# Four streams in place of three in a software-pipelined kernel of eight layers

## The reference

```python
x = x + L0_attn(layernorm(x))   # geo: 8 heads, causal, a geometric term in the scores
x = x + L0_ffn(layernorm(x))    # 8 experts, 128 -> 512 -> 128, relu, the best one by centroid
x = x + L1_attn(layernorm(x))   # "differential": per token, 32x32 scores between its own heads;
                                # itself a block with two norms and a 512-wide feed-forward
x = x + L1_ffn(layernorm(x))    # 128x128 product of values quantised in blocks of 32
x = x + L2_attn(layernorm(x))   # LoRA attention, 16 heads, no mask
x = x + L2_ffn(layernorm(x))    # 14 experts, 128 -> 256 -> 128, gelu, router
x = x + L3_attn(layernorm(x))   # wide: 16 heads with 128-deep q and k, causal
x = x + L3_ffn(layernorm(x))    # 8 experts, 128 -> 128 -> 128, relu, with a capacity
```

## Time and profile before

| what | value |
|---|---|
| median of three runs | 3041.17 us (3022.04 to 3044.92) |
| the profiled execution | 3002.18 us |
| span in its profile, first to last instruction | 3001.0 us |
| instructions | 42829 |
| PE, PEld busy | 2090.2 us (70%), 1445.4 us (48%) |
| DVE, ACT, POOL busy | 1728.2 us (58%), 1143.4 us (38%), 665.1 us (22%) |
| mean granted clock of PE | 0.787 of 2.4 GHz |
| DMA | 200.32 MB, mean 67 GB/s |

### The profile page before, as it was taken

The page is one execution under the profiler, slowest core; times in us unless marked ns, Lnnn a source line. Parts: engine busy times, 40 slices in busy tenths (PEclk is TensorE's granted clock), DMA queues, the critical chain, the costliest instruction groups (busy, mean ns, idle before and its releaser), DMA issues. The chain is left out here.

```text
span 3001.0 us, 42829 instructions
## 1 busy us (share of the span) xinstructions
PE 2090.2 (70%) x13457; PEld 1445.4 (48%) x13457; DVE 1728.2 (58%) x4326; ACT 1143.4 (38%) x2744; POOL 665.1 (22%) x904
## 2 busy tenths in 40 slices
PE   4530775689856895589847895689858895578483
PEld 3330542456443653457444654457445654354352
DVE  2346548565765668465765667465856667453132
ACT  0320432355433553245323553245324552254251
POOL 2015013401251014300250014200250024200101
PEclk9775875699667996789678986789678976897695
DMA  6120141203040313213140313212140503211402
GB/s 179 43 71 0 22 118 36 80 20 116 25 137 15 96 43 92 82 32 104 30 140 7 113 37 95 67 57 80 38 134 1 129 29 90 59 22 33 139 1 59
DMA packets 263737, 200.32 MB, mean 67 GB/s; under 512 B 28708, under 2 KB 236964, under 8 KB 262980
## 3 DMA queue, kind: packets, MB, share of 16 engines
q1 hardware_dynamic: 257348, 184.77, 22.1%
q0 software_dynamic: 6144, 12.60, 1.4%
HBM read 151.18 MB, written 35.49 MB: 62 GB/s over the span
## 5 line engine op out<-in xcount | busy, mean ns | idle before, releaser
L1230 ACT ACTIVATE mid_room<-ps 128x512 f32<-128x512 f32 x256 | 153.1, 598 | 171.9 <-PE ps L940 171.6
L1184 ACT ACTIVATE late_room<-ps 128x384 f32<-128x384 f32 x256 | 125.7, 491 | 210.1 <-PE ps L865 206.7
L1196 ACT ACTIVATE late_room<-ps,late_neg_max 128x128 f32<-128x128 f32 (+1 forms) x512 | 186.7, 420 | 22.2 <-DVE late_neg_max L1566 19.3
L1031 PE MATMUL ps<-mid_pool 128*128 128x128 f32 x544 | 122.4, 361 | 91.2 <-DMA mid_pool<-moe_small 64.9
L1589 DVE TENSOR_REDUCE mid_room<-ps 128x2 f32<-128x512 f32 x256 | 163.8, 686 | 37.2 <-PE ps L927 34.5
L1565 DVE TENSOR_REDUCE late_neg_max<-ps 128x1 f32<-128x128 f32 x256 | 73.9, 289 | 188.8 <-PE ps L857 188.7
L938 PE MATMUL ps<-mid_pool 48*128 48x256 bf16 x512 | 164.9, 322 | 21.1 <-DVE max_rows L1604 20.3
L940 PE MATMUL ps<-max_rows,of_unit 96*128 96x256 bf16 x512 | 166.9, 326 | 0.0
L855 PE MATMUL ps<-late_aT,heads_T 128*128 128x256 f32 x512 | 162.5, 401 | 0.0
L1743 DVE TENSOR_TENSOR early_pool<-ps,early_pool 128x1024 f32<-128x1024 f32 x128 | 150.7, 1219 | 15.5 <-ACT early_pool L1286 11.2
L1268 ACT ACTIVATE mid_room<-ps,mid_pool 128x128 f32<-128x128 f32 x272 | 85.2, 364 | 183.9 <-PE ps L1031 183.4
...
...
## 6 DMA issues: line engine op xcount, KB each, us to landing
mid_pool<-in_m_w_dram SPq DMA_DIRECT2D x272, 128.0 KB, 2.1
early_pool<-m_folded_w SPq DMA_DIRECT2D x88, 256.0 KB, 3.2
early_pool<-in_m_w_dram SPq DMA_DIRECT2D x88, 256.0 KB, 3.1
...
mid_room<-moe_sorted_in SPq DMA_DIRECT2D x32, 256.0 KB, 3.0
moe_sorted_out<-mid_room SPq DMA_DIRECT2D x32, 256.0 KB, 2.4
```

The costliest lines, as they stand in the source:

```text
L1031: mm = pe.matmul(ps[:, B + b % h_banks, c * P:(c + 1) * P], table[:, c * P:(c + 1) * P], rows_T[s][:, b, :], start=True, stop=True)
L1196: ins = act.activation(probs[s][:, n % RING, qt, 0:w], ps[:, bank, qt * P:qt * P + w], ACT.Exp, bias=neg_max[s][:, n % RING, qt:qt + 1])
L1230: act.activation(probs_T[s][:, n % (2 * QUAD), :], ps[:, B + slots.index(("unit", n)) % S_BANKS, :], ACT.Exp)\
```

## The change

Four streams. EARLY keeps the geo attention and `MOE0`; the new SECOND has the differential attention, its feed-forward and the quantised layer; MID keeps LoRA and `MOE2`; LATE is as it was. Banks: EARLY 0 and 1 (one for scores), SECOND 2, MID 3 and 4, LATE 5 to 7. Turns: E, ES, ESM, five of ESML in the loop, SML, ML, L: eleven. New orders of steps are written for each, 313 letters for ESML: 58 of EARLY, 72 of SECOND, 102 of MID, 81 of LATE. Beside it:

- `geo_q` has two tiles with four heads each, like `geo_k`; scores take 17 rows of each at the head's strip. The strip copies and POOL's memset go.
- q, k and v of a tile are copied to SBUF by ACT (ring of three); DVE reads them there, and takes each quarter's reduction right behind its product.
- The values' tile `v_pad` is packed; the last stream's out tiles are placed elsewhere.
- A whole table per expert lies in DRAM; one DMA fetches it, and three tables are in flight. The tables of `MOE2` and `MOE3` are laid out by copies that ACT issues in the preparation; SP waits for them at the end of the first turn.
- The group's input is loaded at the start of the turn in which EARLY takes it; `x_next` goes.
- ACT keeps the values' product of a quad behind the next exponential, not ahead of it.

The diff, cut to its core ("..." marks what is left out):

```diff
-TABLES = 4
-TABLE_DMAS = 3
+TABLES = 3
...
+    def score_banks(self, at):
+        return self.banks if at is LORA else self.banks - 1
...
-EARLY = Stream("early", 0, 3, ["geo_in", "geo_out", "moe0_router", "diff_in", "diff_out"],
-               ["v", "o", "conn"])
-MID = Stream("mid", 3, 2, ["diff_ff", "mx_in", "lora_in", "lora_out", "moe2_in"], ["ff", "mx", "v", "o"])
+EARLY = Stream("early", 0, 2, ["geo_in", "geo_out", "moe0_router"], ["v", "o"])
+SECOND = Stream("second", 2, 1, ["diff_in", "diff_out", "diff_ff", "mx_in"], ["conn", "ff", "mx"])
+MID = Stream("mid", 3, 2, ["lora_in", "lora_out", "moe2_in"], ["v", "o"])
 LATE = Stream("late", 5, 3, ["wide_in", "wide_out", "moe3_router"], ["v", "o"])
-STREAMS = (EARLY, MID, LATE)
-S_BANKS = 2
+STREAMS = (EARLY, SECOND, MID, LATE)
...
+        first_copies = table_copies(MOE0, None, a["m0_w2"], None, a["m0_b2"])
+        later_copies = (table_copies(MOE2, a["m2_w1"], a["m2_w2"], a["m2_b1"], a["m2_b2"])
+                        + table_copies(MOE3, a["m3_w1"], a["m3_w2"], a["m3_b1"], a["m3_b2"]))
...
             @block.scalar
             def _(act):
...
+                act.wait_ge(weights_here, LOADED)
+                for dst, src in later_copies:
+                    with nc.allow_non_contiguous_dma(reason="columns of tables, once"):
+                        act.dma_start(dst, src).then_inc(later_tables, 16)
...
-                    sp.dma_start(tables[s][:, i, 0:m.w2_at], layer1[m][:, bass.ds(expert, 1), :]).then_inc(here, 16)
-                    sp.dma_start(tables[s][:, i, m.w2_at:m.b2_at],
-                                 layer2[m][:, bass.ds(expert * m.chunks, m.chunks), :]).then_inc(here, 16)
-                    sp.dma_start(tables[s][:, i, m.b2_at:m.width],
-                                 small[m][bass.ds(expert * P, P), :]).then_inc(here, 16)
+                    sp.dma_start(tables[s][:, i, :].unsqueeze(1), whole[m][:, bass.ds(expert, 1), :]).then_inc(here, 16)
...
-                if load_from is not None:
-                    sp.dma_start(x_next[:, :, :], load_from).then_inc(x_here, 16)
+                if EARLY in streams:
+                    sp.dma_start(x[EARLY][:, :, :], load_from).then_inc(x_here, 16)
+                    sp.wait_ge(x_here, 16)
...
                 def score_bank(s, at, lag, kind, n):
...
-                    if k >= S_BANKS:
-                        before_kind, before_n = slots[k - S_BANKS]
+                    ring = s.score_banks(at)
+                    if k >= ring:
+                        before_kind, before_n = slots[k - ring]
...
                     def qkv(t):
-                        if t >= 2:
-                            pe.wait_ge(qkv_used, t - 1)
-                        pe.matmul(ps[:, B + t % 2, 0:3 * DIM], aT[s][:, t * P:(t + 1) * P], diff_w[:, :],
+                        if t >= 1:
+                            pe.wait_ge(qkv_kept, t)
+                        pe.matmul(ps[:, B, 0:3 * DIM], aT[s][:, t * P:(t + 1) * P], diff_w[:, :],
...
                     for c in range(DIFF_FF // P):
-                        if c >= 2:
-                            pe.wait_ge(dh_kept, c - 1)
-                        pe.matmul(ps[:, B + c % 2, :], diff_w1[:, c * P:(c + 1) * P], aT[s][:, :],
+                        if c >= 1:
+                            pe.wait_ge(dh_kept, c)
+                        pe.matmul(ps[:, B, :], diff_w1[:, c * P:(c + 1) * P], aT[s][:, :],
...
-                            for rows, h in strips_of(b):
-                                ins = act.activation(geo_q[rows, h, :], ps[rows, B + b % s.banks, :], ACT.Copy)
...
-                    pool.memset(geo_q[:, :, :], 0.0).then_inc(geo_q_free, 1)
...
-                        k = diff_k[:, t % 2, :].rearrange("p (j d) -> p j d", d=DIFF_D).unsqueeze(1)
-                        q = ps[:, B + t % 2, 0:DIM].rearrange("p (i d) -> p i d", d=DIFF_D)
+                        q = diff_qkv[:, t % QKV_RING, 0:DIM].rearrange("p (i d) -> p i d", d=DIFF_D)
+                        k = diff_qkv[:, t % QKV_RING, DIM:2 * DIM].rearrange("p (j d) -> p j d", d=DIFF_D)
...
         with nc.Block(no_gpsimd_drain=True) as block:
-            group_block(block, [EARLY, MID], x_v[:, 2 * TILES:3 * TILES, :],
-                        None)
+            group_block(block, [EARLY, SECOND], x_v[:, TILES:2 * TILES, :], None)
+        next_turn()
+        with nc.Block(no_gpsimd_drain=True) as block:
+            group_block(block, [EARLY, SECOND, MID], x_v[:, 2 * TILES:3 * TILES, :], None)
         next_turn()
         with nc.Fori(0, GROUPS - 3) as g:
             with nc.Block(no_gpsimd_drain=True) as block:
-                group_block(block, [EARLY, MID, LATE], x_v[:, bass.ds(g * TILES + 3 * TILES, TILES), :],
+                group_block(block, list(STREAMS), x_v[:, bass.ds(g * TILES + 3 * TILES, TILES), :],
                             out_v[:, bass.ds(g * TILES, TILES), :])
             next_turn()
         with nc.Block(no_gpsimd_drain=True) as block:
-            group_block(block, [EARLY, MID, LATE], None,
-                        out_v[:, (GROUPS - 3) * TILES:(GROUPS - 2) * TILES, :])
+            group_block(block, [SECOND, MID, LATE], None, out_v[:, (GROUPS - 3) * TILES:(GROUPS - 2) * TILES, :])
```

389 lines of the change are left out of this document (193 added, 196 removed).

## The result

| | before | after |
|---|---|---|
| median, us | 3025.95 (3007.43 to 3047.53, 20 runs) | 3052.55 (3029.11 to 3070.38, 20 runs) |
| ratio, 95% interval | | 1.008 (1.0056 to 1.0098) |
| span of the profiled execution | 3001.0 | 3055.9 |

The account below looks back on a forecast made before the run. No engine was full; DVE's work stood in each turn's last third, when PE's was nearly gone. Preparation and turns summed to 2713 us, 2714 with 1.2 around, scaled by 1.013 to 2750; range 2610 to 2930.

Parts of the forecast that it names:

- E's single bank: First attention's scores wait for the previous unit's exponentials: 20 us in E alone, 5 in ES, nothing in ESML.
- Rival C: Slower: E's single score bank stalls PE in the written order, 75 us a full turn, scaled total 3128; chance 0.05.
- E, 150 forecast: Turn of EARLY alone: chain 123.9, input load 2.7, bank wait 20, turn's end and barrier 3, together 150 us.
- Tables, "nothing": Expert tables held, four to three: fetch lands in 2.1 us, under two blocks, so no cost; 6.8 us if cover goes.
- The full turn, 285 forecast: ESML turn: 1.27 times M's 226.4 us chain is 287, lessened to 285; five make 1425 us.
- ESM, SML, ML: Partial turns around the loop: ESM 248 us, SML 255, ML 226.
- Preparation, 78: Laying out whole tables in DRAM adds 8 us to 70, bounds 0 and 33, as copies may share engines with the store.
- v from SBUF, bounds of 0.1 us: DVE's reads of q, k, v from SBUF: same 1218 ns as PSUM, within 0.1 us each, 2 us a turn either way.
- the chains of M: Stream chain lengths after the change: M 226.4 us, L 152.9, S 142.1.
- FF's single bank: Four feed-forward products lose double buffering: three waits for ACT of about 1 us, 3 us of PE queue, inside the 285.
- B: Full turn stays 325 us, as one written order makes streams wait behind S's DVE pairs; scaled total 2951; chance 0.21.
- Rival A: PE never short of work, clock near full: full turn some 260 us, scaled total 2601; chance 0.17.

Follow-up runs that it names:

- the fourth run: The changed kernel with E on banks 5 to 7, two for scores, in the turns without LATE: 3005.02 against 3039.16 us for the kernel before, ratio 0.9895.
- the best kernel: Changed kernel plus 128-row scores, two E score banks without LATE, v side by side, later tables issued by SP, four tables for MID and LATE: 2821.30 us, ratio 0.931.
- The orders' run: Changed kernel with twelve full ESML turns in six written step orders, each twice, outputs not the reference's: turns of 322.3 to 413.4 us.

## Why the prediction was wrong

By size the step that failed is the length of the full turn, 206 of the 343 us that the trace is over the sum; its cause is in part open. The terms come in the order in which a cause could be shown.

**The missing term: the rows of the scores.** I took "scores take 17 rows of each" as a change of layout, and counted only its gains (the strip copies and the memset). Its cost was on the path: 2.35% in the kernel before, 3.0% the other way in the changed one. The earlier trace rows showed the scores' loop at the full clock with 128-row operands, and I carried the durations over to another form. Of the causes that an edit shows, this is the largest.

**E's single bank, mis-sized.** The mechanism was right, the size not. 16 x 1.26 = 20 us took the loop's times at the full clock; the run gives 35, with the clock at 0.55 in the loop. In it ACT's new order came along; with two banks and full rows that order costs nothing in E (the attention takes 27.7 us with it, 30.0 without). "Nothing in ESML, 5 in ES" was too little as well: giving E its second score bank back made turn E 28 us shorter and ES 13 (1.8% in all). In full turns one bank costs 18 us in an order made for two; in the orders of the change a third bank gave 5.9 in the one pair of turns with it. Rival C's 75 us a turn did not come.

**E, 150 forecast, 179.8 measured:** two parts grew. The attention takes 70.8 us (101.3 to 172.1) for 30.0, 21 more than the 20 that I had counted: bank and rows together. The experts' products take 41.6 (209.7 to 251.3) for 30.0, and with three banks in the fourth run still 39.7, so it isn't the bank. PE waits there for the tables, 13.5 us where it waited 6.5 before:

```profile
L1038 PE MATMUL ps<-early_room,early_pool 128*128 128x128 f32 x88 | 14.6, 316 | 15.5 <-DMA early_pool<-moe_tables 13.5 <-ACT early_room L1276 1.3 <-ACT early_room L1266 0.7
```

Whether one copy for three or three tables for four does it wasn't tried for EARLY. With three banks and full rows the turn is 130.1, 131.0 in the best kernel, beside the sum's 123.9 + 2.7 + 3 = 129.6. That agreement is in part luck: the experts' products still take 40 us in it, and other stretches of the turn are as much shorter.

**Tables, "nothing".** I set the fetch's lead, two blocks, against 2.1 us to land. That duration was of 128 KB; the whole table is 321 KB for mid, 578 KB for early, and in a stretch where three streams' experts run at once the DMA share is 0.55. PE waited 55 us in all for mid's tables, and a fourth table is worth 1.6%. I had named the price of lost cover (6.8 us a turn), and the waiting was nearly that (55.2 over eight turns with mid is 6.9 each). So the DMA wait that one copy for three was to take away came back.

**The full turn, 285 forecast, 326.3 measured.** The step that failed is the scale: 1.27 times the longest chain, kept in check by 212 us of PE's work at 0.85 per us. Both are shares of one turn in one order. After the change PE has the same work (254.4 x 0.84 = 214), M alone is the longest chain with 224.9 (226 was right), and the turn is 1.45 times it. The earlier trace rows was read rightly, DVE's work did stand in the last third; but that it held PE up there was an inference. A third of the thin stretch's PE time is still idle. PE's three longest kinds of wait in the full turn from 1418.7 on (us in all, times, longest us) are for DVE, which gives a stream's tokens to be transposed; the first stands at the turn's start, the other two in the thin stretch:

```profile
PE ps L804 <- DVE mid_z L1494: 11.7, 2, 11.4
PE ps L804 <- DVE second_zz L547: 8.2, 1, 8.2
PE ps L804 <- DVE late_z L1494: 7.6, 1, 7.6
```

Of the 57 us in the thirteen longest kinds 42 are waits for DVE, 4.5 for tables, and the best kernel has the same three on top (11.5, 8.4 and 8.5). Its 307.4 is still 22 over. The orders' run shows 322 to 413 us from the same instructions, and 28 us less of DVE's work or 156 matmuls less give next to nothing, so what is left lies, as far as is known, in who waits behind whom. Which of these waits can be taken out stays open.

**ESM, SML, ML.** ESM, 248 against 290.7 at a clock of 0.63: full rows alone bring it to 270.3, and the best kernel has 259.6 at 0.75. SML 255 against 280.6, with four tables alone 271.9, then 268.6. ML 226 against 236.8: 227.2 in the best kernel, but 237.1 with four tables alone, so the tables aren't shown to be its cause.

**Preparation, 78 against 87.8.** My bounds, 0 and 33, held it. The sum set the copies beside the store, and the store did become late: 14.1 us to land for 7.4 without the copies, and 20.4 for 7.8 for the small one behind it, which sets the end. By the Trainium skill (DMA: Bandwidth & Descriptors, "Issuing engines are not separate DMA queues") SP's store and ACT's copies interleave on the same engines; the trace agrees, with these landings. What I had at nothing is the issuing: the eight issues hold ACT for 52 us, from 27.4 to 79.3, and that alone accounts for some 9 of the 14 us, an estimate from the end of the issues, 79.3, against 70.2, where the small store lands without them.

**v from SBUF, bounds of 0.1 us.** q and k took 1226 ns against 1218, inside the bounds. v took 2048: its view steps by eight elements. Read from PSUM before, the same step took 1225 (line 1772), so it is the step in SBUF that costs. I had used q's row for a form with another stride. 5.6 us a turn of DVE where I allowed 2; the full turns did not show it.

**Right:** the chains of M (226 forecast, 224.9 alone) and L (153, 149.9 in its turn), and roughly that of S (142, 154.4 alone); FF's single bank is not among the thirteen longest kinds of PE waits in a full turn.

**The rivals.** B is nearest to what happened to the full turn: its 325 against 326.3, its sign, waits of all streams for DVE, and its mechanism, one written order, which the runs of orders bear out. But not through S's pairs as I put it (halving them gives 0 to 10 us), so that the number fits so well is luck. Its total of 2951 was short because the partial turns lost too. Rival A's hope, a clock near 1.0, did not come: the clock is 0.80 to 0.84 in the full turns shown, and 0.774 over the span for 0.787 before. The Trainium skill's sentence beside it (TensorE: Matmul & The Clock Gate, "What's actually happening": the slow clock is the default, activity lifts it) agrees with the trace where PE idles (E with one bank) and doesn't tell of the stretch that decided here, 0.53 at 95% busy.
